# Q projection over two pairs of images at once, tokens turned three pairs ahead

## The reference

```python
h = h + attn(layernorm(h))      # 16 heads of 16, linear attention:
    Q, K = elu(x@Wq.T + bq) + 1, elu(x@Wk.T + bk) + 1;  V = x@Wv.T + bv
    KV = K^T V per head;  Z = 1 / (Q . sum(K) + 1e-6);  out = (Q KV Z) @ Wo.T + bo
h = h + ffn(layernorm(h))       # 8 experts, top 1, gated by a sigmoid
```

## Time and profile before

| | us |
|---|---|
| median of 3 runs | 459.18 (457.03 to 460.8) |
| the profiled execution, its own time | 458.15 |
| its span, first to last instruction | 456.3 |
| PE / DVE / POOL / ACT busy in the span | 434.4 / 331.1 / 293.4 / 262.2 |
| loop of 32 steps, about | 49.6 to 330 |
| experts, about | 340 to 456 |

### The profile page before, as it was taken

One profiled execution on the slowest core, in us unless ns is written; L12 is line 12 of the kernel. 1 busy time (PEld: TensorE's weight loads), 2 busy tenths in 40 slices (PEclk: granted clock), 3 DMA queues, 4 the chain that ended last, 5 costly groups with the idle time before them and its releaser, 6 DMA issues.

```text
span 456.3 us, 11809 instructions
## 1 busy us (share of the span) xinstructions
PE 434.4 (95%) x3746; PEld 413.1 (91%) x3746; DVE 331.1 (73%) x1115; ACT 262.2 (57%) x640; POOL 293.4 (64%) x662
## 2 busy tenths in 40 slices
PE   8999999999999999999999999999779999999990
PEld 8999999999999999999999999899767888888870
DVE  5669469989989988988988998997575444444440
ACT  6444566766766766766765775675425454544430
POOL 4155223877777877777778777676557756565663
PEclk9999999999999999999999999999799999999996
DMA  8972221333231121133112112057214892212120
GB/s 305 350 226 85 61 55 51 103 85 101 76 102 51 60 79 53 36 97 103 38 48 58 38 43 74 25 153 223 81 51 128 260 294 89 89 61 77 56 85 14
DMA packets 34142, 46.37 MB, mean 102 GB/s; under 512 B 8842, under 2 KB 25856, under 8 KB 34082
## 3 DMA queue, kind: packets, MB, share of 16 engines
q1 hardware_dynamic: 24860, 30.50, 21.9%
q0 software_dynamic: 9216, 15.12, 10.6%
q10 hardware_dynamic: 6, 0.00, 0.0%
HBM read 26.87 MB, written 17.17 MB: 97 GB/s over the span
## 4 chain that ended last, share of the span: by engine, by line
PE 90%; issue 3%; DVE 3%; POOL 1%; ACT 1%; POOLq 0%; DVEq 0%
PE b_kg L1584 11%; PE b_w L1328 7%; PE b_w L1329 7%; PE b_w L1330 6%; PE b_att L1441 6%; PE b_kg L1328 5%; PE b_kg L1329 5%; PE b_kg L1330 5%; PE b_att L1380 4%; PE b_t L1393 4%; PE b_v L1330 3%; PE b_v L1328 3%; PE b_v L1329 3%; PE b_att L1620 3%; PE b_w L1620 3%
## 5 line engine op out<-in xcount | busy, mean ns | idle before, releaser
L658 POOL DMA_INDIRECT sorted_rows<-rows,place x64 | 75.6, 1181 | 20.3 <-issue 9.7
L736 POOL DMA_INDIRECT out<-result,rows_all x64 | 62.4, 974 | 36.5 <-DVE result L1258 24.4
L1584 PE MATMUL b_kg<-wgu,xsT 128*128 x256 | 66.1, 381 | 0.1
L1247 DVE SCALAR_TENSOR_TENSOR act_u<-b_kg,rows_all,silu_g 128x128 f32<-128x128 f32 x64 | 19.5, 346 | 57.1 <-ACT silu_g L915 57.1
L1584 PEld LDWEIGHTS b_kg<-wgu,xsT 128*128 128x128 f32 x256 | 43.8, 190 | 3.8 <-issue 0.2
L831 ACT ACTIVATE q_exp<-b_w,bq_s 128x228 f32<-128x228 f32 x64 | 28.9, 452 | 29.7 <-PE b_w L1330 29.7
L1328 PE MATMUL b_w<-wo_hi,attnT_hi 128*114 128x264 f32 x124 | 40.9, 330 | 0.0
L1328 PE MATMUL b_kg<-wkgv_hi,xnT_hi 128*114 128x264 f32 x128 | 38.7, 302 | 0.7 <-DVE patch_out L986 0.7
L1328 PE MATMUL b_w<-xnT_hi,wq_hi 128*128 128x256 f32 x128 | 38.5, 301 | 0.7 <-DVE logits L1069 0.6
L1441 PE MATMUL b_att<-kv_sb,qT 128*114 128x136 f32 x256 | 35.9, 284 | 1.9 <-issue 1.9
L1329 PE MATMUL b_kg<-wkgv_lo,xnT_hi 128*114 128x264 f32 x128 | 36.5, 285 | 0.0
(11 more groups left out here) (223 smaller groups left out, 1469.8 us busy)
## 6 DMA issues: line engine op xcount, KB each, us to landing
rows_all<-sorted_rows SPq DMA_DIRECT2D x64, 130.0 KB, 3.1
rows_all<-in_x SPq DMA_DIRECT2D x18, 384.0 KB, 4.5
rows_all<-in_txt SPq DMA_DIRECT2D x32, 154.0 KB
wgu<-in_wgu_in SPq DMA_DIRECT2D x8, 256.0 KB, 3.0
rows_all<-patch_out SPq DMA_DIRECT2D x48, 36.0 KB
sorted_rows<-tail_rows SPq DMA_DIRECT2D x9, 130.0 KB, 2.2
sorted_rows<-rows,place POOLq DMA_INDIRECT x64, 3.7
wdown<-in_wdown_in SPq DMA_DIRECT2D x2, 512.0 KB, 4.4
```

Of the source, the lines that this page charges most:

```text
L658: G.indirect_dma_start(out=scratch[0:EXPERTS * REGION, :], out_offset=bass.IndirectOffsetOnAxis(ap=place[:, k, b:b + 1], axis=0), in_=rows ...
L736: G.indirect_dma_start(out=out, out_offset=bass.IndirectOffsetOnAxis(ap=rows_all[:, t.n, ID:ID + 1].bitcast(I32), axis=0), in_=result[:, k ...
L1247: last = V.scalar_tensor_tensor(act_u[:, t.slot(4)], b_gu[m.slot(2)][:, up:up + INNER], rows_all[:, t.n, GAIN:GAIN + 1], silu_g[:, t.slot( ...
L1584: last = T.matmul(to, xsT[:, t.slot(6), k, :], wgu[:, bass.ds(e, 1), k, :], start=(k == 0), stop=(k == KC - 1))
```

## The change

One projection of queries now works for a group of two pairs (456 columns, no padding) and makes half of the features: `queries(h)` is for half c = h % 2 of the features of group h // 2, with 6 matmuls of 456 columns in the place of 12 of 256. It stands at the same place of each engine's step, but as `queries(i+1)` in step i, since a group's second half must be there for the first of its pairs. So that both pairs of a group are at hand, tokens are normalised and turned three pairs ahead (`normalised(i+3)`, `turn_tokens(i+3)`, `tokens_high(i+3)`, `tokens_low(i+3)`, `stats_1(i+4)`, `rstd1_of(i+4)`); `xnT_hi`, `xnT_lo` and `qT` hold two groups. Step 0 is written out so that it turns pair 2 and makes half 0 between K and V, and pair 3 and half 1 at its end. In DVE's step `tokens_low` now stands behind `stats_2`, where it stood ahead of it. More of the first pairs' work goes between the units.

```diff
-QW = 256
+GROUP = 2
+QW = GROUP * 2 * TOK
...
-            qT = sb("qT", [P, KC, 2 * TOK], at=room)
+            qT = sb("qT", [P, 2, KC, QW], at=room)
...
+        def of_pair(ring, p):
+            first = p % GROUP * 2 * TOK
+            return ring[:, p // GROUP % 2, :, first:first + 2 * TOK]
...
 ACT step(i)
-                if 0 <= i + 1 < PAIRS:
-                    normalised(i + 1)
+                if i != 0 and 0 <= i + 3 < PAIRS:
+                    normalised(i + 3)
                 if 0 <= i:
                     keys(i)
+                if i == 0:
+                    tokens_high(2)
+                    queries(0)
+                    normalised(3)
+                if 0 <= i:
                     values(i)
...
-                if 0 <= i + 1 < PAIRS:
-                    tokens_high(i + 1)
-                if 0 <= i:
-                    queries(i)
+                if i != -1 and 0 <= i + 3 < PAIRS:
+                    tokens_high(i + 3)
+                if 0 <= i < PAIRS - 1:
+                    queries(i + 1)
...
 DVE stats_1(p)
+                if 1 <= p <= 5:
+                    dve.wait_ge(mv1_ready, p)
...
 DVE step(i)
-                if 0 <= i - 1:
-                    queries(i - 1)
-                if 0 <= i + 2 < PAIRS:
-                    stats_1(i + 2)
+                if i == 0:
+                    keys(0)
+                    tokens_low(2)
+                if 0 <= i:
+                    queries(i)
+                if 0 <= i + 4 < PAIRS:
+                    stats_1(i + 4)
...
                 if 0 <= i - 1:
                     attention(i - 1)
-                if 0 <= i + 1 < PAIRS:
-                    tokens_low(i + 1)
                 if 0 <= i - 2:
                     stats_2(i - 2)
+                if 0 <= i + 3 < PAIRS:
+                    tokens_low(i + 3)
...
 DVE, list of the units
-                gate_centred, 10, 11, gate_columns, 12, lambda: weight_low(0), 13, lambda: weight_low(1), lambda: step(-2), 14,
-                lambda: weight_low(2), 15, 16, 17, lambda: step(-1), room_setup])
+                gate_centred, 10, 11, gate_columns, 12, lambda: weight_low(0), 13, lambda: weight_low(1), lambda: stats_1(0), 14,
+                lambda: weight_low(2), lambda: stats_1(1), 15, 16, 17, lambda: tokens_low(0), lambda: stats_1(2),
+                lambda: tokens_low(1), room_setup, lambda: stats_1(3)])
...
 PE turn_attention(p)
-                pe.wait_ge(xnT_lo_ready, min(p + 3, PAIRS))
+                pe.wait_ge(xnT_lo_ready, min(p + 5, PAIRS))
...
 PE queries
-                for c in range(KC):
-                    for k in range(KC):
-                        w = slice(c * P, (c + 1) * P)
-                        last = product(b_w[:, c, 0:QW], (wq_hi[:, k, w], wq_lo[:, k, w]),
-                                       (xnT_hi[:, p % 2, k, :], xnT_lo[:, p % 2, k, :]), k == 0, k == KC - 1)
+                w = slice(c * P, (c + 1) * P)
+                for k in range(KC):
+                    last = product(b_w[:, c, 0:QW], (wq_hi[:, k, w], wq_lo[:, k, w]),
+                                   (xnT_hi[:, g % 2, k, :], xnT_lo[:, g % 2, k, :]), k == 0, k == KC - 1)
...
 PE step(i)
                 if 0 <= i:
-                    project(i)
+                    project_keys(i)
+                if i == 0:
+                    turn_tokens(2)
+                    queries(0)
+                if 0 <= i:
+                    project_values(i)
...
-                if 0 <= i + 1 < PAIRS:
-                    turn_tokens(i + 1)
-                if 0 <= i:
-                    queries(i)
+                if i != -1 and 0 <= i + 3 < PAIRS:
+                    turn_tokens(i + 3)
+                if 0 <= i < PAIRS - 1:
+                    queries(i + 1)
...
 PE, list of the units
-                             *range(11, 17), lambda: early_step(-1), 17])
+                             *range(11, 16), lambda: early_step(-3), 16, lambda: early_step(-2), 17])
```

More of the change, by code:

```diff
@@ L204, in build @@
         with ExitStack() as room:
-            q_exp = sb("q_exp", [P, KC, 2 * TOK], at=room)
-            q_relu = sb("q_relu", [P, KC, 2 * TOK], at=room)
-            qT = sb("qT", [P, KC, 2 * TOK], at=room)
+            q_exp = sb("q_exp", [P, QW], at=room)
+            q_relu = sb("q_relu", [P, QW], at=room)
+            qT = sb("qT", [P, 2, KC, QW], at=room)
             k_exp = sb("k_exp", [TOK, 2, D], at=room)
@@ L667, in step @@
                     scatter(i - 4)
-                if 0 <= i + 2 < PAIRS:
-                    rstd1_of(i + 2)
+                if 0 <= i + 4 < PAIRS:
+                    rstd1_of(i + 4)
                 if 0 <= i - 3:
@@ L712, in _ @@
             bias_parts(slice(D, KGW))
+            step(-4)
+            step(-3)
             step(-2)
@@ L715, in _ @@
             pool.wait_ge(s_const, 16 * CONST_DMAS)
-            pool.wait_ge(s_posb, 2)
+            pool.wait_ge(s_posb, 1)
             pool.wait_ge(patches_ready, PT)
@@ L819, in tokens_high, with queries @@
                 act.wait_ge(turn_done, p + 1)
[L820 to L828, removed]
-                for c in range(KC):
[L830 to L833, removed]
+                if p >= 4:
+                    act.wait_ge(q_done, p - 2)
+                S.copy(of_pair(xnT_hi, p), turned()).then_inc(xnT_hi_ready, 1)
+            def queries(h):
+                c = h % KC
+                act.wait_ge(q_done, h + 1)
+                if h >= 1:
+                    act.wait_ge(q_ready, h)
+                S.activation(q_exp[:], b_w[:, c, 0:QW], ACT.Exp, bias=bq_s[:, c:c + 1])
+                S.activation(q_relu[:], b_w[:, c, 0:QW], ACT.Relu, bias=bq_s[:, c:c + 1]).then_inc(q_parts, 1)
             def step(i):
@@ L899, in _ @@
             act.wait_ge(s_small, 16 * SMALL_DMAS)
+            step(-3)
+            step(-2)
             step(-1)
@@ L963, in position @@
             def position():
[L965 to L968, removed]
                 dve.wait_ge(s_pos, 16)
@@ L1025, in tokens_low @@
                 dve.wait_ge(xnT_hi_ready, p + 1)
-                low(xnT_lo[:, p % 2, :, 0:2 * TOK], turned(), xnT_hi[:, p % 2, :, 0:2 * TOK]).then_inc(xnT_lo_ready, 1)
+                low(of_pair(xnT_lo, p), turned(), of_pair(xnT_hi, p)).then_inc(xnT_lo_ready, 1)
             def attention_low(p):
@@ L1040, in masked, with queries @@
                                 ALU.mult).then_inc(kv_ready, 1)
[L1042 to L1047, removed]
+            def queries(h):
+                g = h // KC
+                dve.wait_ge(q_parts, h + 1)
+                if g >= 2:
+                    dve.wait_ge(apply_done, GROUP * (g - 1))
+                V.scalar_tensor_tensor(qT[:, g % 2, h % KC], q_exp[:], 1.0, q_relu[:], ALU.min, ALU.add).then_inc(q_ready, 1)
             def keys(p):
@@ L1187, in step @@
                     attention_low(i - 2)
-                if 0 <= i - 1:
-                    queries(i - 1)
-                if 0 <= i + 2 < PAIRS:
-                    stats_1(i + 2)
+                if i == 0:
[3 more added lines that the diff above has]
+                    queries(i)
+                if 0 <= i + 4 < PAIRS:
+                    stats_1(i + 4)
                 if 0 <= i - 3:
                     route(i - 3)
-                if 0 <= i:
+                if 0 < i:
                     keys(i)
@@ L1297, in _ @@
             attention_low(PAIRS - 2)
-            queries(PAIRS - 1)
             route(PAIRS - 3)
@@ L1394, in turn_attention, with tokens_of, project_keys @@
                 last.then_inc(turn_attn_done, 1)
-            def project(p):
-                k_, tokens = p % 2, [slice(b * TOK, (b + 1) * TOK) for b in range(2)]
+            def tokens_of(p, b, k):
+                at = slice(b * TOK, (b + 1) * TOK)
+                return of_pair(xnT_hi, p)[:, k, at], of_pair(xnT_lo, p)[:, k, at]
+            def project_keys(p):
                 pe.wait_ge(xnT_lo_ready, p + 1)
@@ L1405, in project, with project_values @@
                     for k in range(KC):
-                        last = product(to, (xnT_hi[:, k_, k, tokens[b]], xnT_lo[:, k_, k, tokens[b]]),
-                                       (wkgv_hi[:, k, 0:KGW], wkgv_lo[:, k, 0:KGW]), k == 0, k == KC - 1)
+                        last = product(to, tokens_of(p, b, k), (wkgv_hi[:, k, 0:KGW], wkgv_lo[:, k, 0:KGW]), k == 0, k == KC - 1)
                 last.then_inc(kg_done, 1)
+            def project_values(p):
                 if p >= 1:
@@ L1413, in project @@
                     for k in range(KC):
-                        last = product(to, (xnT_hi[:, k_, k, tokens[b]], xnT_lo[:, k_, k, tokens[b]]),
-                                       (wkgv_hi[:, k, KGW:], wkgv_lo[:, k, KGW:]), k == 0, k == KC - 1)
+                        last = product(to, tokens_of(p, b, k), (wkgv_hi[:, k, KGW:], wkgv_lo[:, k, KGW:]), k == 0, k == KC - 1)
                 last.then_inc(kvp_done, 1)
@@ L1420, in project_out @@
```

(32 more changed lines are left out.)

## The result

The changed kernel takes 476.22 us in the median of 4 runs (474.32 to 477.48), the kernel before 459.89 beside it: ratio 1.036, 95% interval 1.030 to 1.042. The forecast was 475.5, with a range of 461 to 480. The profiled execution took 476.43 us, its span is 474.4 against 456.3, so 18.1 us are to be found.

What follows compares the result with a forecast made beforehand. Two equal bounds were seen, PE's list and the chain from `apply` to `rank`, each 1.81 us. Profiled 458.15 + 13.9 stalls + 3.0 start = 475.05, with half the median's difference 475.5 us; range 461 to 480.

Steps and rivals of the forecast that it cites:

- The step that decides: Steady step: late `tokens_low` holds bank `b_t`, so `turn_attention` stalls 0.54 us and the period becomes 9.19.
- The gain: Steady step on PE: list 0.20 us shorter, but `rank` still waits for `attention`, so gain 0 (between 0 and 0.03).
- The chain: From `apply` over denominators, reciprocal and attention to `rank`: 1.81 us, as long as PE's list there, a second bound.
- Rival C: PE's list the only bound, exchange covered: 455.5 us, or 441.5 at the lower matmul bound; chance 0.06.
- A matmul of 456 columns: Query projection on PE: taken as 0.200 us, between bounds 0.117 and 0.208, so a half costs 1.28 against 1.48.
- The stalls: PE ahead of `turn_attention` in 27 steps: 25 x 0.54 + 2 x 0.2 = 13.9 us.
- the two late ones: Stalls of steps 28 and 29, where DVE was already late by itself: 0.2 us each.
- The start: Work before the steady loop, for the deeper lead: 3.0 us more, between 1 and 4.
- the wait for xn of pair 3: Step 0: `turn_tokens(3)` waits for `normalised(3)`, which ACT runs behind `queries(0)`; 1.0 us, between 0 and 2.
- unit 15's wait: Start, on DVE: statistics of pair 1 ahead of unit 15's low part; 0.45 us, between 0 and 0.94.
- the half microsecond: Half of the 1.0 us by which the median of runs exceeded the profiled execution, taking 475.05 to 475.5 us.
- its rival, 441.5 us: Whole kernel: PE's list alone bounds and a matmul costs 0.117 at any width; shares a chance of 0.06.

Runs made afterwards that it cites:

- Run 1: `low_first`: the changed kernel with `tokens_low` put back ahead of `stats_2` in DVE's step, nothing else undone; 462.23 us, ratio 1.008 to the kernel before.
- run 2: The kernel before with only `stats_2` moved ahead of `tokens_low` in DVE's step; 473.12 us, ratio 1.031.
- Run 3: The kernel before without the `xnT_lo` x `wq_hi` query products, 8 matmuls a step for 12; 457.76 us, ratio 0.998.
- Runs 4 and 7: 4: `low_first` plus first image's K ahead of `rank`, `stats_1` ahead of `masked`, 459.15 us; 7: 4 without `xnT_lo` x `wq_hi` query products, 444.68 us.
- run 5: The kernel before with first image's K ahead of `rank` and `stats_1` ahead of `masked`, queries unchanged; 474.11 us, ratio 1.034.

## Why the prediction was right

**The step that decides held.** "`turn_attention` is released at 1.45 ... due at 0.90": its weights were loaded at 1.42 and it ran from 1.46. The period came out at 9.18 for the 9.19 forecast. Run 1 takes the exchange out of the change and gets 8.65 back; run 2 puts it alone into the kernel before and gets 9.18. That the lead of three pairs would not help, since the wait is for the bank and not for the data, is what run 1 and run 2 show together.

**The gain was hidden as said.** The chain and PE's list had the same length. Run 3 shows the chain as a bound: 0.47 us less of list, nothing gained. Runs 4 and 7 show the list as the other one: with the chain covered, 0.13 and 0.41 us came off, as much as the matmuls had saved. Rival C's ground, a chain that is 90% PE, was true of the listing and wrong as a price. For the kernel before itself the length of the list alone stays argued, since run 5 made another loop.

**Terms that were off.** A matmul of 456 columns takes 0.206 us in the steady steps, not 0.200: 0.82 for four in the timeline above (201.17 to 201.99), the same over 19 steps. (The 0.209 in the expectations is from the first pairs.) From `rank` back, the half starts at -1.44 and leaves PE free at -0.33 + 0.21 = -0.12: 1.32 us for 1.48, but begun 0.04 later than the queries before, which started at -1.48. PE is early by 0.12, where I had said 0.20. The term was nearer to its upper bound, 0.208, than to the value taken; it had no effect on the time, being hidden. The stalls: 25 x 0.54 + 2 x 0.2 = 13.9 were forecast. `low_first` differs from the changed kernel by the exchange alone; against it the 28 periods are 13.5 longer (255.95 for 242.48) and step 3 is 0.8 longer, 14.3 together. The first stall was thus larger than the others (0.76 us by the listing; step 3 has no `rank` yet), and the two late ones cost 0.31 and 0.36 for the 0.2 that I took.

Against the kernel before, the 28 periods are only 12.1 longer, since the rest of the change gave 1.3 back where the prediction had put nothing: the four periods that end at the `rank` of steps 27 to 30 take 34.9 us in `low_first` and 36.2 in the kernel before, 8.67 for 9.53 in the one of step 29. DVE ran late there, and with tokens three pairs ahead it has no `stats_1` after step 27, where it had them up to step 29. That fits, but no run takes it apart. The start: forecast 3.0, measured 3.3, of which the wait for xn of pair 3 was 0.82 for my 1.0, unit 15's wait 0.37 for my 0.45.

So the sum was 16.9, and stalls, start and that gain come to 16.3. The 1.1 us of early delay in this execution and 0.7 us behind the loop, neither of them forecast, filled up the rest, as the half microsecond did that I had added for the median; a part of the close agreement is luck.

**The page named in the prediction.** The Trainium skill, TensorE: Matmul & The Clock Gate, "Back-to-back issue gap", gives 131 ns for 512 columns in a stream. Here 456 columns took 206. The measurement decides; its rival, 441.5 us, had also needed both waits gone.

## What to carry to other kernels

Before an engine's list is shortened, find how late the others release its next wait: an engine that is 100% busy by the listing may already be standing for a chain of equal length, and then the saving turns into a wait. Look up what a wait protects: tokens that are ready three pairs ahead don't help where the wait is for the bank in which they are turned, and an item of 0.94 us put in front of its last reader cost about 0.53 us in each of 27 steps (14.3 in all). No run gave the attention transposes a bank of their own, which would test the bank from the other side. A deeper lead pays only with a second move that uses it, here K work ahead of `rank`, together with an order on the other engine that fits it.

## What the runs showed of the hardware

Fewer weight loads gave next to nothing here, at the full granted clock (1.00 from 85 to 262 us). One load for 456 columns in the place of one for 256 left the cost nearly in proportion to the columns: 0.117 us for 256 and 0.206 for 456, 0.457 and 0.452 ns a column. Twelve and six of them make 1.40 and 1.24, and of this 0.17 the padding alone, 456 columns for 512, is 11% of 1.40 or 0.15.
